# One unit per row group in a graph kernel's transposed copy: the diagonal as an ordinary unit, ten unit places, and loads that wait for their own store

## The reference, cut to what matters

```python
# N = 4096 nodes, 128 features, adj is 4096 x 4096 f32
h  = relu(layernorm(x))
d  = 1 / sqrt(sum(adj, -1))
z  = leaky_relu(d * (adj @ (d * h)) @ W1 + b1)
S  = exp(-dist(z, z) / 2), kept for the 4 nearest of each row only
A2 = S + adj
d2 = 1 / sqrt(sum(A2, -1))
x1 = x + d2 * (A2 @ (d2 * h)) @ W2 + b2
h2 = relu(layernorm(x1))
out = x1 + h2 @ W_self.T + (adj @ h2) @ W_neigh.T + b
```

## Time and profile before

| | |
|---|---|
| median of 3 runs | 1305.23 us (1304.32 to 1310.51) |
| the profiled execution, its own time | 1303.21 us |
| its span in the trace | 1301.2 us |
| busy | PE 934.7, DVE 888.0, POOL 657.8, ACT 597.3 us |
| first part | from the start to about 412 us |
| second part | from about 412 to about 540 us |
| moved by DMA | 357.73 MB, mean 275 GB/s |

### The profile page before, as it was taken

One profiled execution on the slowest core, in us unless ns is written; L12 is line 12 of the kernel. 1 busy time (PEld: TensorE's weight loads), 2 busy tenths in 40 slices (PEclk: granted clock), 3 DMA queues, 4 the chain that ended last, 5 costly groups with the idle time before them and its releaser, 6 DMA issues.

```text
span 1301.2 us, 13552 instructions
## 1 busy us (share of the span) xinstructions
PE 934.7 (72%) x3570; PEld 664.9 (51%) x3570; DVE 888.0 (68%) x852; ACT 597.3 (46%) x1105; POOL 657.8 (51%) x936
## 2 busy tenths in 40 slices
PE   0132154474776999899999994666777777799998
PEld 0111022232333444477777773455666666588886
DVE  1966665654554321288999999937777777788885
ACT  0533343162460322255555555635555554567673
POOL 9798779877820000044444444588888887200000
PEclk9985676786987999899999998788888888899999
DMA  9999999999996975295444445695777777599993
GB/s 222 323 349 367 363 343 382 349 365 351 354 374 230 357 266 187 92 262 200 158 157 157 155 157 206 184 379 203 282 279 271 284 274 273 215 358 384 381 382 124
DMA packets 117253, 357.73 MB, mean 275 GB/s; under 512 B 34528, under 2 KB 59872, under 8 KB 89568
## 3 DMA queue, kind: packets, MB, share of 16 engines
q1 hardware_dynamic: 60896, 273.11, 55.2%
q0 software_dynamic: 47104, 80.00, 20.6%
q10 hardware_dynamic: 9216, 4.20, 1.2%
HBM read 250.02 MB, written 106.95 MB: 274 GB/s over the span
## 4 chain that ended last, share of the span: by engine, by line
PE 31%; POOL 21%; DMA 18%; issue 14%; DVE 11%; ACT 2%; SPq 1%; POOLq 0%; DVEq 0%; ACTq 0%
DMA araw<-in_adj_dram 15%; POOL zt_lo L576 11%; PE ps L1157 7%; POOL araw L365 7%; PE ps L1274 4%; PE ps L1275 4%; PE ps L1276 4%; PE ps L1252 2%; PE ps L1253 2%; PE ps L1254 2%; PE ps L1255 2%; DVE m L988 2%; DVE bmax L975 2%; DVE i L990 2%; POOL t_st L505 1%
## 5 line engine op out<-in xcount | busy, mean ns | idle before, releaser
L365 POOL DMA_DIRECT2D araw<-in_adj_dram x512 | 301.1, 597 | 66.4 <-ACTq L637 26.9
L1018 DVE TENSOR_TENSOR araw_r<-araw,tr_r 128x2048 fp32r<-128x2048 f32 x128 | 289.4, 2296 | 44.6 <-ACT tr_r L731 44.4
L731 ACT ACTIVATE tr_r<-araw 128x2048 fp32r<-128x2048 f32 x128 | 241.7, 1911 | 66.2 <-PE ps L1276 37.9
L576 POOL DMA_INDIRECT zt_lo<-neighbour_table,idx_st x128 | 193.9, 1515 | 45.7 <-issue 39.2
L714 ACT ACTIVATE araw<-ps,nsq 128x1024 f32<-128x1024 f32 x128 | 142.5, 1117 | 115.3 <-PE ps L1255 96.0
L1274 PE MATMUL ps<-araw_r,zt_hi 128*128 128x512 f32 x256 | 110.2, 430 | 93.2 <-DVE araw_r L1018 63.9
L633 ACT ACTIVATE ps<-araw 128x256 f32<-128x256 f32 x304 | 111.1, 365 | 59.4 <-DMA araw<-in_adj_dram 55.3
L886 DVE TENSOR_REDUCE part<-araw 128x16 f32<-128x4096 f32 x13 | 57.4, 4413 | 98.1 <-DMA araw<-in_adj_dram 98.1
L1252 PE MATMUL ps<-sq_rows,pick 128*128 128x512 f32 x256 | 102.3, 400 | 17.7 <-POOL zs_lo L493 10.8
L1274 PE MATMUL ps<-araw_r,ys_r 128*128 128x512 f32 x256 | 101.7, 397 | 9.5 <-DVE araw_r L1018 9.5
L1274 PEld LDWEIGHTS ps<-araw_r,zt_hi 128*128 128x128 f32 x256 | 52.1, 204 | 109.5 <-DVE araw_r L1018 69.4
(11 more groups left out here) (150 smaller groups left out, 1654.7 us busy)
## 6 DMA issues: line engine op xcount, KB each, us to landing
araw<-transposed SPq DMA_DIRECT2D x152, 1024.0 KB, 6.2
araw<-in_adj_dram POOLq DMA_DIRECT2D x512, 128.0 KB, 21.2
keys_scratch<-araw SPq DMA_DIRECT2D x64, 512.0 KB, 4.2
transposed<-tr SPq DMA_DIRECT2D x28, 1024.0 KB, 9.0
transposed<-unit_zt_hi SPq DMA_DIRECT2D x18, 1024.0 KB, 8.7
transposed<-unit_zt_lo SPq DMA_DIRECT2D x18, 1024.0 KB, 9.4
xs<-in_x_dram SPq DMA_DIRECT2D x64, 64.0 KB, 2.1
araw<-transposed SPq DMA_DIRECT2D x8, 512.0 KB, 7.4
```

Source lines behind the costliest of these rows:

```text
L365: gp.dma_start(araw[R * q + first:R * q + R:SPREAD, c], adj_v[q, first:R:SPREAD, g // 2, g % 2, :, c]).then_inc(a_first_in[c], DMA)
L576: gp.indirect_dma_start(out=gath[:, i, u, k, :], out_offset=None, in_=table, in_offset=bass.IndirectOffsetOnAxis(ap=idx_st[:, i, u * TOPK ...
L731: act.activation(ring_hi[:, place % TSLOTS], ring[:, j], ACT.Copy).then_inc(hi_done, 1)
L1018: v.tensor_tensor(ring_lo[:, j], ring[:, j], ring_hi[:, place % TSLOTS].bitcast(F32), ALU.subtract).then_inc(lo_done, 1)
```

## The change

A unit becomes (g, j): the four tiles of row group j, so tile i of it is i * 8 + j. Every unit is then wholly below, on or above the diagonal.

- The diagonal (g, g) is an ordinary unit: the extra transpose, its own place in `tr` and its two semaphores are gone, and `diagonal` multiplies from the unit place. Slots of `araw` no longer wait for `diag_ready`.
- `UT` is ten: all four places of `tr` and two more in `sq_rows`. The zeros that DVE wrote at the start into the lower half of `sq_rows` are now written by GpSimd at the end of its loads, after the last two units in those places have been stored and used.
- `units_b` has 28 units, all of 1 MB. Each load waits for its own unit's store, not for all of them. SP waits for all stores later, ahead of the loads of the second product.
- The counts that PE waits for in the third product change from `j // 2 * 2 + 3` to `j + 2`.

```diff
-        units_z = [... for z in ("zt_hi", "zt_lo")]
+        units_z = [... for z in ("zt_hi", "zt_lo", "sq_rows")]
...
-        units_t = [tr[:, i] for i in range(TSLOTS - 1)] + [z[:, i] for z in units_z for i in range(2)]
+        units_t = [tr[:, i] for i in range(TSLOTS)] + [z[:, i] for z in units_z for i in range(2)]
...
+        units_a = [(g, j) for g in range(GROUPS) for j in range(GROUPS)]
+        LATE = [U <= g < GROUPS - 1 for g in range(GROUPS)]
...
+        units_b = [(g, j) for g in reversed(range(GROUPS - 1)) for j in range(g + 1, GROUPS)]
+        B_IN = [sum(n % GROUPS == i for n in range(len(units_b))) * DMA for i in range(GROUPS)]
...
                 if n >= SLOTS:
                     gp.wait_ge(t_ready, CHUNK_UNITS * (n - SLOTS + 1))
-                    gp.wait_ge(diag_ready, diagonals[n - SLOTS])
...
                 else:
-                    sp.wait_ge(t_used, TILES_A + sum(len(u[-1]) for u in units_b[:n - GROUPS + 1]))
-                src = at[g, c * CHUNK_UNITS + half].rearrange("p (t k) -> p t k", t=U)
-                sp.dma_start(ring[:, slot, 0:len(tiles)], src[:, tiles[0] - half * U::tiles.step]).then_inc(a_in[slot], DMA)
+                    sp.wait_ge(t_used, TILES_A + U * (n - GROUPS + 1))
+                stored = g * GROUPS + j
+                sp.wait_ge(at_out[stored % UT], (stored // UT + 1) * DMA)
+                sp.dma_start(flat(ring[:, slot]), at[g, j]).then_inc(a_in[slot], DMA)
...
             for n in range(len(units_a)):
                 keep_unit(n)
-            for i in range(UT):
-                sp.wait_ge(at_out[i], STORED[i])
             for n in range(len(units_b)):
                 load_upper(n)
...
             load_first(gp)
+            for i in range(UT - 2, UT):
+                gp.wait_ge(at_out[i], STORED[i])
+                last = max(n for n in range(len(units_a)) if n % UT == i and used_after[n])
+                gp.wait_ge(t_used, used_after[last])
+            gp.memset(sq_rows[2 * R:P].bitcast(F32), 0.0).then_inc(sq_clear, 1)
+            gp.wait_ge(sq_clear, 1)
...
             def keep_partial(g):
-                act.wait_ge(diag_used, g + 1)
+                act.wait_ge(t_used, used_after[g * GROUPS + g])
...
-            v.memset(sq_rows[2 * R:P].bitcast(F32), 0.0)
...
-                transposed(units_t[n % UT], c, half * UNIT_COLS, U).then_inc(t_ready, 1)
+                src = araw[:, j // CHUNK_UNITS].rearrange("p m (t h s) -> p h t m s", h=CHUNK_UNITS, s=R)[:, j % CHUNK_UNITS]
+                v.transpose(units_t[n % UT].rearrange("p t (m s) -> p t m s", s=R), src).then_inc(t_ready, 1)
...
-                if c == g // 2:
-                    if g >= 1:
-                        v.wait_ge(diag_used, g)
-                    own = araw[:, c].rearrange("p m (t h s) -> p h t m s", h=2, s=R)[:, g % 2]
-                    v.transpose(tr[:, TSLOTS - 1].rearrange("p t (m s) -> p t m s", s=R), own).then_inc(diag_ready, 1)
...
             def diagonal(g):
-                pe.wait_ge(diag_ready, g + 1)
                 pe.wait_ge(y_ready, g + 1)
-                for cc in range(CHUNKS):
-                    ins = pe.matmul(acc[g % 2], ys[:, cc * GROUPS + g], tr[:, TSLOTS - 1, cc],
-                                    start=g == 0 and cc == 0, stop=cc == CHUNKS - 1)
-                ins.then_inc(diag_used, 1)
+                n_u = g * GROUPS + g
+                first_unit(t_ready, n_u + 1, units_t[n_u % UT], g, g % 2, g == 0, True)
...
-                pe.wait_ge(kept, j // CHUNK_UNITS * 2 + 3)
+                pe.wait_ge(kept, j + 2)
```

More of the change, by code:

```diff
@@ L270, in gnn_kernel @@
         UNITS = GROUPS * GROUPS
-        def tile_at(c, place):
-            return place // 2 * GROUPS + 2 * c + place % 2
         def by_unit(tiles):
-            of = tiles.rearrange("p (v w a h) f -> p a v w h f", v=2, w=2, a=CHUNKS, h=2)
-            return [of[:, j // CHUNK_UNITS, j % CHUNK_UNITS] for j in range(GROUPS)]
-        def usable(g, c, half):
-            if c < g // 2:
-                return range(half * U, half * U + U)
-            return range(half * U, half * U + U, 2) if c == g // 2 and g % 2 else range(0)
@@ L299, in gnn_kernel @@
-        for g in reversed(range(GROUPS - 1)):
-            for c in range((g + 1) // 2, CHUNKS):
-                for half in range(CHUNK_UNITS):
-                    own = c == g // 2
-                    units_b.append((g, c, half, range(half * U + own, half * U + U, 1 + own)))
-        assert len(units_b) % GROUPS == 0
-        B_IN = len(units_b) // GROUPS * DMA
-        USED1 = TILES_A + sum(len(u[-1]) for u in units_b)
+            of = tiles.rearrange("p (u g) f -> p g u f", g=GROUPS)
+            return [of[:, j] for j in range(GROUPS)]
@@ L328, in gnn_kernel @@
         for g in F1[1:]:
-            ends.append(ends[-1] + CHUNKS * (GROUPS - 1 - g))
+            ends.append(ends[-1] + U * (GROUPS - 1 - g))
         LAG = 7
@@ L339, in gnn_kernel @@
         SPLIT_SQ = [t + 2 + LAG for t in STAGE_C]
-        LATE = [U <= g < GROUPS - 1 for g in range(GROUPS)]
-        def late_diag(g, c, half):
-            return g >= 0 and LATE[g] and c == 0 and half == 0
         def wait_alone(eng, signal, value):
@@ L857, in _ @@
             v.scalar_tensor_tensor(negmr[:], mv[:, :, 0], -1.0, tmp32[:], ALU.mult, ALU.mult).then_inc(ln_ready, 1)
-            def transposed(out, slot, off, tiles):
-                src = araw[:, slot, :, off:off + tiles * R].rearrange("p m (t s) -> p t m s", s=R)
-                return v.transpose(out.rearrange("p t (m s) -> p t m s", s=R), src)
             def unit(n):
-                g, c, half, _ = units_a[n]
+                g, j = units_a[n]
                 if n >= UT:
```

86 lines of the change are left out of this document (44 added, 42 removed).

## The result

Timed beside each other on one chip, the changed kernel takes 1311.18 us (median of 20 runs, 1301.95 to 1313.29) and the kernel before 1303.38 us (median of 20 runs, 1295.88 to 1310.51). The ratio is 1.0053, 95% interval 1.0034 to 1.0071: slower, by some 7 us (the medians differ by 7.8), where I had forecast 2 us less. The change does what it was written to do: SP's first load is early. What stands behind it is late.

The account below looks back on a forecast made before the run. The first part was taken as bound by DMA, so only the hand-over to the second part counted: 2.0 us gained at stage B, all else 0, giving 1301.2 us (1303.2 on the median's footing), range 1297 to 1307.

Parts of the forecast that it names:

- What bounds the first part: First part, up to the last reduction: bound by DMA, matrix loads and unit stores end to end, together 385 of 395 us.
- Rival A: First part gets shorter through the transposes on the chain: 6.8 us there, 8.8 in all, 1296.4 us; chance 0.11.
- Extra transposes: DVE in the first part: eight diagonal transposes fewer, 18.2 us of DVE work, taken as 0 gain, at most 6.8 us.
- their new pattern: Transposes reading every second run of 32 columns: 2274 ns against 2288 for the old pattern, cost 0.
- ten places: Ten unit places instead of seven in the first part: DVE never waited for a store, so 0.
- `kept`: Changed counts PE waits for in the third product: the data is ready before PE needs it, cost 0.
- End of the first part: Hand-over: ys ready 2.27 us earlier, at 409.7; diagonal ends at 415.0, a gain of 0.8 hidden unless the load is there.
- Loads that wait for their own store: Start of second part: SP's first load issued 3.9 us earlier, at 408.2; PE starts on it at 415.3 instead of 417.20.
- What is late next: Before stage B: last four hw_scratch stores land at 421.7, 12.4 us after first issue; z ready at 423.6, gain 2.0 us.
- rival B: The last hw_scratch stores land at 424.6 and hold up z: stage B 0.9 us later than before, 1306.1 us; chance 0.10.
- The rule that I took from the Trainium skill: DMA queues served in turn: each 64 KB store waits for about one 1 MB load, landing by 421, gain 2.2 us.
- Rival D: GpSimd's zeros, a memset of 10 us, hold up DVE's last reduction: up to 5 us, net 3 slower, up to 1308.2; chance 0.04.

Follow-up runs that it names:

- a2_all_stores: The changed kernel, but SP again waits for all stores before the second part's first load, as before the change; 1300.34 us, ratio 0.9995.
- a3_eight_places: The changed kernel with eight unit places instead of ten, none in sq_rows; 1306.47 us, ratio 1.0035 to the kernel before.
- a4_filled_wait: The changed kernel with four unused matmuls put ahead of the first stage B to keep PE busy while it waits for z; 1309.08 us, ratio 1.0053.
- b1: The kernel before with only the own-store waits added: each second-part load waits for its own unit's store; 1307.82 us, ratio 1.0039.
- a5_early_loads: The changed kernel with the last hw_scratch part staged in out_t and SP's first four second-part loads ahead of the last two stores; 1299.43 us, ratio 0.998.
- a0_again: The changed kernel, unedited, run and profiled again; 1306.4 us, ratio 1.0036 to the kernel before.
- a0_third: The changed kernel, unedited, a single execution for a third profile; 1311.63 us.
- a0_fourth: The changed kernel, unedited, a single execution for a fourth profile; 1308.18 us.

## Why the prediction was wrong, step by step

- *What bounds the first part*: right. Full DMA engines, the same waits for the matrix; the last reduction moves by several us between executions of either kernel. Rival A (the first part gets shorter) gave nothing.
- *Extra transposes, their new pattern, ten places, `kept`*: 0 within what can be told, as forecast. a2_all_stores holds all of them together at 0.9995 (0.9974 to 1.0016); a3_eight_places shows the places alone.
- *End of the first part*: `ys` 10.7 us behind the reduction, as forecast; the diagonal ends 14.5 behind in the first profile and 15.7 to 16.8 behind in the other three of this kernel (forecast 16.0), with the first load used 17.1 behind in all four.
- *Loads that wait for their own store*: right in kind. Issued 9.4 us behind the reduction (forecast 9.2), used 17.1 behind (forecast 16.3, before 18.2): a gain of 1.1 instead of 1.9. The last store, with loads behind it now, took 5.6 us to land instead of 4.2, so the first load found less of a head start than I had counted. In the first profile PE then needed 5.35 us for the unit instead of 3.67, since its clock had fallen behind the 2.59 us of waiting, and was ready for stage B at 26.8; in the other three it was ready at 25.1 (forecast 24.4).
- *What is late next*: the step that failed. I named the right transfer and took 12.4 us from first issue to last landing; 17.2 were measured, beyond even the upper bound of 15.3. With it the gain of 2.0 us at stage B became a loss of 2.4. I had built the 12.4 as 1.6 us for a store that meets idle engines and four spacings of 2.7. But no store meets idle engines any more: the first one issued took 8.6 us. The other three landed behind it at a mean spacing of (17.2 - 8.6)/3 = 2.9 us, so the spacing was about right and the start was wrong. The upper bound was no bound: I took it from group 2 alone, whose 15.3 us is the second shortest of the seven groups of the first part, and group 0 of the same trace took 18.9. The argument against rival B, that only SP's queue is beside these stores, was no argument: with SP's queue alone, full of 1 MB loads, they took 17.2 us, within the 15.1 to 18.9 that they took beside SP's and GpSimd's queues in the first part. The rule that I took from the Trainium skill, page "DMA: Bandwidth & Descriptors", section "Queues, rings and completion order", each engine taking a packet from each queue in turn, gave a landing by 421, 22 us behind the reduction; it came at 27.5. The measurement decides: as I applied it, the rule gives too little for a small store behind a full queue. What the page has in turn are packets; that a store waits for one whole 1 MB load was my own reading of it.
- *The term that was left out*: TensorE's clock. I counted a wait as its own length. In the changed kernel the wait of 2.9 to 4.5 us ahead of stage B was followed by stretches at or near the lower level that come to 7 to 10 us, and a4_filled_wait puts the price at 2.3 us at the distances (its total does not show it). Late landing and lower clock make 4.9 us at the distances; rival B had 0.9.
- *Rival D, GpSimd's zeros*: refuted. From the timeline of the kernel after:

```profile
389.26 3.51 POOL L509 MEMSET sq_rows<- 64x4096 f32 x1 [17.94 <-DMA transposed<-unit_sq_rows]
```

  It took 3.51 us, not up to 10, and ended ahead of the last reduction. No profile shows a reduction beside it, so whether the two would hold each other up is not tested here. Beside it DVE did two transposes in 4.51 us, their usual length.
- *The range*: 1297 to 1307 held neither the 1311.18 nor the ratio of 1.0053, which on the footing of 1305.23 is 1312. It was made from scatter and a B of +0.9; B at its measured size, 4.9, would have reached 1310.

What stays open: why the stores land after 17.2 us in the changed kernel and after 12.6 in b1, where SP's first load is 3.1 us ahead of them instead of 0.9 (the head start alone is not it: in a5_early_loads four loads are issued from 5.9 us ahead, and they take 17.2 again; half of b1's first eight loads are of 512 KB and its stores are issued within 1.6 us instead of 2.5, neither of which was tried alone); why b1 and a4 are 1.004 and 1.005 in all, when at the distances they are 1.7 and 2.6 us behind the kernel before (means of their profiles); where the 2 us lie by which the changed kernel's first comparison (1.0053) exceeds the 4.9 us at the distances; and what decides in a given run whether the keys' stretch takes its short form or a longer one. The profiles of b1 and a4 all lie in the longer ones (558.2 to 559.8 to the third product), but a0_again's and a3's lie in the short one and those kernels are slower too, so 16 single profiles don't settle it.

## What to carry to other kernels

When a queue is allowed to start earlier, ask which small transfer used to slip through the gap that it leaves, and who waits for it; if it is read from a tile that is about to be written again, give it a tile of its own (here that alone turned 1.0036 into 0.9976). Take a bound from every row that shows the case and not from one of them. Look at what TensorE's clock does behind a wait, too, and not at the wait's length alone (here 2.1 to 3.1 us more up to the distances, though the total of a4_filled_wait didn't follow). Compare kernels by landmarks that count from the same event, over several profiles, before a difference at the end is given a cause.

## What the runs showed of the hardware

- Four stores of 64 KB, issued on ACT's queue within 3 us and just behind the first of ten 1 MB loads on SP's queue, took 8.6 to 14.7 us each to land; with SP held back (a2_all_stores) they took 1.8 to 3.0 us.
- In the changed kernel TensorE's waits of 2.9 to 4.5 us ahead of stage B were followed by the lower clock in all four profiles, and the way to the distances took 2.1 to 3.1 us longer than the 115.6 us before. Later, near 620 us, a wait of 2.31 us was followed by it in one profile (a0_third) and not in another (a0_fourth).
- GpSimd's memset of 64x4096 f32 took 3.51 us, beside an estimate of up to 10.
- Within the changed kernel's 20 first runs the mean granted clock goes with the time: 0.880 in the median at 1311 us, and 0.886 in the one run of 1301.95. It does not rank kernels: a4_filled_wait's runs had 0.8835 in the median and took 1309.08 us, a2_all_stores's 0.885 and 1300.34.
